# Expert 0's layer 1 in halves of the slots, and vector work reordered around the first gathers, in a routed expert kernel

## What is computed

```
probs  = softmax(rot(x) @ gate_w.T)                 # 4096 x 8; rot mixes the four 128-wide parts of a token
keep   = tokens that pick expert e (top-p 0.9), and that are among the 512 best of e by rank
h      = gelu(rot(x)[kept] @ w1[e].T)               # 512 slots x 512
y      = h @ w2[e].T                                # 512 slots x 512
out    = x + sum over e of probs[:, e] * y[e]       # only for kept tokens
```

## Time and profile before

| | |
|---|---|
| median of 3 runs | 282.74 us (281.26 to 282.98) |
| profiled execution, its own time | 284.87 us |
| its span, first to last instruction | 283.1 us |
| PE busy in the span | 244.9 us, 87% |
| DVE busy | 208.1 us, 74% |
| ACT busy | 151.8 us, 54% |
| POOL busy | 144.5 us, 51% |
| mean granted clock of TensorE | 0.916 of full speed |

### The profile page before, as it was taken

How to read it: one execution, slowest core, us unless ns; L and a number is a source line. 1 busy time by engine, 2 the same in 40 slices (tenths; PEclk the granted TensorE clock), 3 DMA queues, 4 the chain that set the end, 5 groups by cost and what they waited for, 6 DMA issues and landing times.

```text
span 283.1 us, 3852 instructions
## 1 busy us (share of the span) xinstructions
PE 244.9 (87%) x1326; PEld 183.9 (65%) x1326; DVE 208.1 (74%) x505; ACT 151.8 (54%) x281; POOL 144.5 (51%) x104
## 2 busy tenths in 40 slices
PE   0868858665489999999999999999999999999980
PEld 0645423212248888788888888888888888888760
DVE  5299977998955897799789779869977966951330
ACT  6331205686134774676587377468657746754200
POOL 0000000000877258858867885885888587583521
PEclk9995868675759999999999999999999999999997
DMA  6999989910348026925973792594498259054520
GB/s 233 426 424 416 495 306 389 335 47 2 111 128 356 3 74 211 263 48 147 320 128 86 289 220 47 170 300 83 111 312 171 77 208 162 8 77 67 148 111 37
DMA packets 12482, 53.38 MB, mean 189 GB/s; under 512 B 2720, under 2 KB 2976, under 8 KB 9248
## 3 DMA queue, kind: packets, MB, share of 16 engines
q1 hardware_dynamic: 4208, 35.31, 34.1%
q0 software_dynamic: 8256, 17.85, 28.0%
HBM read 44.63 MB, written 17.96 MB: 221 GB/s over the span
## 4 chain that ended last, share of the span: by engine, by line
PE 73%; DVE 13%; DMA 4%; ACT 3%; issue 3%; POOL 2%; POOLq 0%; SPq 0%; ACTq 0%; DVEq 0%
PE bank L762 21%; PE bank L763 20%; PE bank L764 20%; PE bank L742 4%; PE bank L824 2%; ACT region L405 2%; DVE xg L589 2%; DMA xg<-in_x,gath 2%; DMA region<-in_xt 2%; DVE region L637 2%; POOL xg L255 1%; PE bank L803 1%; PE bank L758 1%; DVE csum L595 1%; DVE rank L593 1%
## 5 line engine op out<-in xcount | busy, mean ns | idle before, releaser
L255 POOL DMA_INDIRECT xg<-in_x,gath x32 | 51.7, 1617 | 97.4 <-DVE gath L525 69.9
L469 DVE SCALAR_TENSOR_TENSOR w1rot<-w1raw,rot,w1rot 128x512 f32<-128x512 f32 x84 | 63.1, 751 | 5.1 <-ACT w1rot L308 3.1
L270 POOL DMA_INDIRECT out<-ysb,scat x32 | 53.8, 1680 | 19.8 <-DVE ysb L711 8.0
L762 PE MATMUL bank<-w2h,hh 128*128 128x512 f32 x128 | 51.7, 404 | 0.0
L762 PE MATMUL bank<-xh,w1h 128*128 128x512 f32 x128 | 50.9, 398 | 0.0
L763 PE MATMUL bank<-xl,w1h 128*128 128x512 f32 x128 | 50.1, 391 | 0.0
L764 PE MATMUL bank<-w2h,hl 128*128 128x512 f32 x128 | 50.0, 391 | 0.0
L764 PE MATMUL bank<-xh,w1l 128*128 128x512 f32 x128 | 50.0, 390 | 0.0
L763 PE MATMUL bank<-w2l,hh 128*128 128x512 f32 x128 | 49.9, 390 | 0.0
L498 DVE TENSOR_TENSOR hl<-hf,hh 128x512 fp32r<-128x512 f32 x32 | 22.0, 689 | 32.5 <-ACT hh L339 32.5
L335 ACT ACTIVATE hf<-bank 128x512 f32<-128x512 f32 x32 | 19.1, 598 | 40.2 <-PE bank L764 40.2
(11 more groups left out here) (128 smaller groups left out, 331.5 us busy)
## 6 DMA issues: line engine op xcount, KB each, us to landing
region<-in_xt SPq DMA_DIRECT2D x8, 1024.0 KB, 9.1
w1raw<-in_w SPq DMA_DIRECT2D x8, 1024.0 KB, 9.1
w2raw<-in_w SPq DMA_DIRECT2D x8, 1024.0 KB, 4.8
xg<-in_x,gath POOLq DMA_INDIRECT x32, 3.7
score<-probs_scratch,pidx POOLq DMA_INDIRECT x32, 2.8
out<-ysb,scat POOLq DMA_INDIRECT x32, 7.2
ch<-in_ch SPq DMA_DIRECT2D x1, 368.5 KB, 7.8
cf<-in_cf SPq DMA_DIRECT2D x1, 149.0 KB, 2.2
```

Source lines behind the costliest of these rows:

```text
L255: pool.indirect_dma_start(xg[:, s, :], None, x_d, bass.IndirectOffsetOnAxis(gath[:, e, s:s + 1], 0)).then_inc(xg_in[s], 16)
L270: pool.indirect_dma_start(out_d, bass.IndirectOffsetOnAxis(scat[:, e, s:s + 1], 0), ysb[:, s, :], None, compute_op=ALU.add if e < LAST els ...
L469: ins = nc.vector.scalar_tensor_tensor(dst, w1raw[:, e % 2, i, :], rot[:, j, i:i + 1], dst, ALU.mult, ALU.add)
L762: nc.tensor.matmul(dst, ah, bh, start=first, stop=False)
```

## The change

Layer 1 of expert 0 becomes four calls of `layer1_half(n)`: halves 0 and 1 take the slots 0 to 255 (gathers 0 and 1) with the hidden parts 0, 1 and 2, 3, halves 2 and 3 the slots 256 to 511. Each is 24 matmuls with 256 moving columns where `layer1` had 12 with 512. The transposes of gather 3 are put behind half 0 on PE, `count_before(1, 2, E)` behind half 1, `slot_rows(2)` behind half 3. The seven `keep_clock` matmuls become two behind gather 0 and two behind gather 1. On ACT `x_high0(3)` stands behind `hidden(0, 0)` and `rows_out(1, ...)` behind `hidden(0, 1)`. On DVE `slot_tables` writes gath three instructions earlier with a semaphore of its own (`gath_ready`), one quarter of w1's low part is put ahead of `slot_tables(0)`, the first three `x_low0` go ahead of `count_tokens(2, E)`, `x_low0(3)` behind it and ahead of `w2_low(0)`, and within expert 0 each step of `rotate_w1` and the slot work of expert 2 is put one place later among the `h_low`. Experts 1 to 7 keep their order. The dtypes, the number of columns times weights, and the bytes moved are the same.

```diff
--- before.py
+++ after.py
@@ -171,6 +171,11 @@
         pbank, lbank, rbank = bank[1:3], [bank[i] for i in (0, 3, 5, 7)], bank[4]
         fbank, kbank, cbank, obank, dbank = [bank[i] for i in (6, 0, 3, 5)], bank[7], bank[1:3], bank[3], bank[7]
 
+        HALF = CAP // 2
+        halved = lambda a, n: a[:, 2 * (n % 2):2 * (n % 2) + 2, HALF * (n // 2):HALF * (n // 2 + 1)]
+        tiled = lambda a, e, n: halved(a, n) if e == 0 else a[:, n, :]
+        paired = lambda a, e: a.rearrange("p (f n) -> p f n", f=2) if e == 0 else a
+
         starts_of = lambda n, e0, e1: (obank[:, 0:2 * (e1 - e0)] if n == 0 else
                                        dbank[:, 512 - 2 * (e1 - e0):512]).rearrange("p (e m) -> p e m", m=2)
 
@@ -190,7 +195,7 @@
         base_ready, tb_mm = sem("base_ready"), sem("tb_mm")
         incl_ready, off_mm, rows_mm, rows_ready, begin_ready = (
             sem(n) for n in ("incl_ready", "off_mm", "rows_mm", "rows_ready", "begin_ready"))
-        after_ready, v_mm, slots_ready = (sem(n) for n in ("after_ready", "v_mm", "slots_ready"))
+        after_ready, v_mm, gath_ready, slots_ready = (sem(n) for n in ("after_ready", "v_mm", "gath_ready", "slots_ready"))
         xg_in = [sem(f"xg_in{i}") for i in range(S4)]
         score_in = [sem(f"score_in{i}") for i in range(2)]
         xt_mm, x_hi, x_lo = sem("xt_mm"), sem("x_hi"), sem("x_lo")
@@ -248,7 +253,7 @@
         @block.gpsimd
         def _(pool):
             def gather_x(e):
-                pool.wait_ge(slots_ready, e + 1)
+                pool.wait_ge(gath_ready, e + 1)
                 if e >= 1:
                     pool.wait_ge(xt_mm, C4 * e)
                 for s in range(S4):
@@ -256,6 +261,7 @@
                                             bass.IndirectOffsetOnAxis(gath[:, e, s:s + 1], 0)).then_inc(xg_in[s], 16)
 
             def gather_scores(e):
+                pool.wait_ge(slots_ready, e + 1)
                 if e >= 2:
                     pool.wait_ge(y_ev, S4 * (e - 1))
                 for s in range(S4):
@@ -336,7 +342,7 @@
                 act.wait_ge(h_act, n + 1)
                 if e >= 1:
                     act.wait_ge(y_mm, S4 * e)
-                nc.scalar.activation(hh[:, f, :], hf[:, n % 2, :], ACT.Copy).then_inc(h_hi, 1)
+                nc.scalar.activation(tiled(hh, e, f), paired(hf[:, n % 2, :], e), ACT.Copy).then_inc(h_hi, 1)
 
             def y_out(e, s):
                 n = S4 * e + s
@@ -417,17 +423,20 @@
             w2_high(0)
 
             nc.scalar.activation(warm[:, :], cfv("ident")[:, 0:1], ACT.Gelu)
-            for s in range(S4):
-                if s == S4 - 1:
-                    rows_out(1, 2, E)
-                x_high0(s)
+            x_high0(0)
+            x_high0(1)
             w1_first(1, 0)
+            x_high0(2)
             for e in range(E):
                 more = e + 1 < E
                 hidden(e, 0)
+                if e == 0:
+                    x_high0(3)
                 if more:
                     w1_first(e + 1, 1)
                 hidden(e, 1)
+                if e == 0:
+                    rows_out(1, 2, E)
                 if more:
                     w1_high(e + 1, 0)
                 hidden(e, 2)
@@ -495,7 +504,7 @@
             def h_low(e, f):
                 n = F4 * e + f
                 dve.wait_ge(h_hi, n + 1)
-                nc.vector.tensor_tensor(hl[:, f, :], hf[:, n % 2, :], hh[:, f, :].bitcast(FP32),
+                nc.vector.tensor_tensor(tiled(hl, e, f), paired(hf[:, n % 2, :], e), tiled(hh, e, f).bitcast(FP32),
                                         ALU.subtract).then_inc(h_lo, 1)
 
             def slots_after(e):
@@ -517,12 +526,11 @@
                                              cfv("slot").unsqueeze(2).to_broadcast([P, S4, NT]), ALU.is_le))
                 then(nc.vector.tensor_reduce(tabg[:, :], before_slot[:, :, :], AX.X, ALU.add))
                 then(nc.vector.tensor_tensor(tabf[:, :], tabg[:, :], vbank[:, :, NT], ALU.add))
-                nc.vector.scalar_tensor_tensor(tabx[:, :], tabf[:, :], float(N), cfv("slot"), ALU.is_ge, ALU.mult)
+                nc.vector.tensor_scalar(gath[:, e, :], tabf[:, :], float(N - 1), None, ALU.min).then_inc(gath_ready, 1)
                 then(nc.vector.tensor_scalar(tabg[:, :], tabf[:, :], float(N - 1), None, ALU.min))
-
-                nc.vector.tensor_tensor(scat[:, e, :], tabf[:, :], tabx[:, :], ALU.add)
                 nc.vector.tensor_scalar(pidx[:, e, :], tabg[:, :], float(E), float(e), ALU.mult, ALU.add)
-                nc.vector.tensor_copy(gath[:, e, :], tabg[:, :]).then_inc(slots_ready, 1)
+                then(nc.vector.scalar_tensor_tensor(tabx[:, :], tabf[:, :], float(N), cfv("slot"), ALU.is_ge, ALU.mult))
+                nc.vector.tensor_tensor(scat[:, e, :], tabf[:, :], tabx[:, :], ALU.add).then_inc(slots_ready, 1)
 
             def count_tokens(e0, e1):
 
@@ -662,31 +670,39 @@
             count_tokens(0, 2)
             nc.vector.tensor_copy(rows[:, :, :, NT], chv("rowbase").unsqueeze(1).to_broadcast([P, E, 2])).then_inc(rows_ready, 1)
             slots_after(0)
+            w1_low(0, 2, 3)
             slot_tables(0)
             slots_after(1)
-            w1_low(0, 2, C4)
+            w1_low(0, 3, C4)
             slot_tables(1)
+            x_low0(0)
+            x_low0(1)
+            x_low0(2)
             count_tokens(2, E)
+            x_low0(3)
             w2_low(0)
-            for s in range(S4):
-                x_low0(s)
 
 
             for e in range(E):
                 more, later = e + 1 < E, e + 2 < E
                 if e >= 1:
                     w2_low(e)
-                if more:
+                if e >= 1 and more:
                     rotate_w1(e + 1, 0)
-                if later:
+                if e >= 1 and later:
                     slots_after(e + 2)
                 h_low(e, 0)
                 if more:
+                    rotate_w1(e + 1, 1 if e >= 1 else 0)
+                h_low(e, 1)
+                if e >= 1 and later:
+                    slot_tables(e + 2)
+                if e == 0:
+                    slots_after(e + 2)
                     rotate_w1(e + 1, 1)
-                h_low(e, 1)
-                if later:
+                h_low(e, 2)
+                if e == 0:
                     slot_tables(e + 2)
-                h_low(e, 2)
                 if more:
                     rotate_w1(e + 1, 2)
                 h_low(e, 3)
@@ -742,15 +758,12 @@
                         last = nc.tensor.transpose(xbank[j % 2][:, s * P:(s + 1) * P], xg[:, s, j * P:(j + 1) * P], ident)
                     last.then_inc(xt_mm, 1)
 
-            def transpose_x0():
-
-                for s in range(S4):
-                    pe.wait_ge(xg_in[s], 16)
-                    for j in range(C4):
-                        last = nc.tensor.transpose(x0bank(s)[:, j, :], xg[:, s, j * P:(j + 1) * P], ident)
-                    last.then_inc(xt_mm, 1)
-                    if s == S4 - 2:
-                        count_before(1, 2, E)
+            def transpose_x0(s):
+
+                pe.wait_ge(xg_in[s], 16)
+                for j in range(C4):
+                    last = nc.tensor.transpose(x0bank(s)[:, j, :], xg[:, s, j * P:(j + 1) * P], ident)
+                last.then_inc(xt_mm, 1)
 
             def keep_clock(n):
 
@@ -766,8 +779,6 @@
             def layer1(e, f):
                 if f == 0:
                     pe.wait_ge(w1_lo, C4 * (e + 1))
-                    if e == 0:
-                        pe.wait_ge(x_lo, S4)
                 n = F4 * e + f
                 if n >= 2:
                     pe.wait_ge(h_act, n - 1)
@@ -779,6 +790,24 @@
                                          xh[:, j, :], xl[:, j, :], j == 0, j == C4 - 1)
                 last.then_inc(h_mm, 1)
 
+            def layer1_half(n):
+
+                if n == 0:
+                    pe.wait_ge(w1_lo, C4)
+                    pe.wait_ge(x_lo, S4 // 2)
+                if n == 2:
+                    pe.wait_ge(x_lo, S4)
+                if n >= 2:
+                    pe.wait_ge(h_act, n - 1)
+                ns = slice(HALF * (n // 2), HALF * (n // 2 + 1))
+                for i in range(2):
+                    f = 2 * (n % 2) + i
+                    fs = slice(f * P, (f + 1) * P)
+                    for j in range(C4):
+                        last = split_product(hbank[n % 2][:, i * HALF:(i + 1) * HALF], w1h[0][:, j, fs], w1l[0][:, j, fs],
+                                             xh[:, j, ns], xl[:, j, ns], j == 0, j == C4 - 1)
+                last.then_inc(h_mm, 1)
+
             def layer2(e, s):
                 if s == 0:
                     pe.wait_ge(w2_lo, e + 1)
@@ -787,7 +816,10 @@
                     pe.wait_ge(y_ev, n - 1)
                 ss = slice(s * P, (s + 1) * P)
                 for f in range(F4):
-                    if s == 0:
+                    if e == 0:
+                        if f == 0:
```

(30 more changed lines are left out.)

## The result

The changed kernel takes 287.09 us (median of 4 runs, 284.4 to 287.86), the kernel before in the same comparison 282.64 (281.26 to 282.98): a ratio of 1.0133, 95% interval 1.0076 to 1.0189. The forecast was 283.2 with a range of 280.6 to 286.1. Three further comparisons, on the chips 8, 0 and 14, gave 1.0098 [1.0067, 1.0128], 0.9927 [0.9903, 0.995] and 0.9935 [0.9905, 0.9965]. So the sign differs between the comparisons, each of them on a chip of its own, and both have to be explained: why it is slower where before stands at 283 us, and why it is faster where before stands at 286.4. The ratios are estimated from the single runs and differ a little from the quotients of the medians (1.0157 here, inside the interval). Runs over 1.5% above the fastest of the same kernel (three took 413, 600 and 1327 us) are left out of the ratios, not of the medians.

What follows compares the result with a forecast made beforehand. PE was taken as the bound once layer 1 of expert 0 has begun, with its lead mostly waited away on DVE. A 0.4 us gain and 0.85 for a clock fall gave 282.74 + 0.45 = 283.2 us, range 280.6 to 286.1.

Steps and rivals of the forecast that it cites:

- part 1: POOL's gathers of expert 0 start 0.43 us earlier; the four land at 73.9, 75.2, 76.7 and 77.8, not 80.6 for the last.
- part 2: On PE, layer 1 of expert 0 starts with half 0 at 77.7, 7.0 us earlier than before.
- part 3: PE's 96 matmuls of 256 columns take 0.121 us each; half 0 ends near 82.75, PE is done at 92.8.
- the rival of exposed weight loads: 256-column matmuls on PE can't hide their weight loads: 4.0 to 5.0 us slower than before, 287.2; chance 0.12.
- The clock's rise at 82.3: During half 0, PE's clock rises near 82.3, counting only the matmuls from 77.7.
- the early case of the text: PE's clock rises as early as 78.7 if all earlier work counts; half 0 ends 1.6 us sooner, gain up to 1.3.
- part 4: DVE's gapless list of 13.92 us puts `x_low(1, 0)` at 98.62; PE waits, keeping 0.4 of its 3.5 us lead.
- part 5: With moved loads beside them, expert 1's gathers land at 94.4 to 96.6; at 95.0, about 2.2 us of PE's idle time.
- part 6: PE's clock may fall in the roughly 3 us wait between 92.8 and 99.3: price 0 to 2.45, taken as 0.85.
- POOL held by `w2_low(0)`: POOL's second gather of expert 1 stands behind DVE's `w2_low(0)`, 85.3 to 87.6; the last is issued near 90.2.
- Sum: Whole kernel: -0.4 for the lead plus 0.85 for the clock makes +0.45, 283.2 us (span 283.5).

Runs made afterwards that it cites:

- e1: Changed kernel with the loads of w2 (expert 1) and w1 (expert 2) held until two transposes of expert 1 are done: 282.76 us, ratio 0.9974.
- r3: The changed kernel again, unedited, on chip 8 beside the kernel before: 286.25 us, ratio 1.0098.
- r4: The changed kernel again, unedited, on chip 14 beside the kernel before: 284.58 us, ratio 0.9935.
- e4: Changed kernel with `w2_low(0)` ahead of `x_low0(0)` on DVE and the loads released one transpose earlier, after gather 2: 278.48 us, ratio 0.9831.
- e7: Changed kernel with the w1 load for expert 2 issued first, after three transposes, and the w2 load behind it: 282.27 us, ratio 0.9872.
- e2: Changed kernel with 24 unused `keep_clock` matmuls behind `slot_rows(2)`, filling PE's wait: 284.31 us, ratio 1.0014.
- e6: Changed kernel with `w2_low(0)` as four 128x512 instructions instead of one 128x2048: 282.94 us, ratio 0.9868.
- b1: The kernel before, unedited, on chip 8 for a second profile: 282.9 us, ratio 0.9991.
- e8: e4 with `w2_low(0)` also cut in four pieces as in e6, against the kernel before on chip 8: 280.51 us, ratio 0.99.
- r1: The changed kernel again, unedited, on chip 0 beside the kernel before: 284.19 us, ratio 0.9927.

## Why the prediction was wrong

- **Gathers of expert 0 (part 1): right in the main.** Transposes at 73.41, 74.91 and 76.67 (said: 73.9, 75.2, 76.7 to 76.85). No gather was held, the first neither: 0.94 to 1.12 us each, where the text gave the first 1.6.
- **Layer 1 starts at 77.7 (part 2): right**, 77.53 (77.73 by the chain).
- **A step of 0.121 (part 3): right**, 0.12; the rival of exposed weight loads fell.
- **The clock's rise at 82.3: wrong.** It rose at about 78.3, the early case of the text. Half 0 was over at 80.80 and not 82.75, and PE done at 90.8 and not 92.8. It rose 0.7 us behind the first matmul of layer 1, with transposes and `keep_clock` ahead of it; e1, r3 and r4, which are the same up to there, have it 0.3 ahead of that matmul to 1.2 behind. The text's reason, that in before it rose only at 85.5 and not in the stretches with gaps, leaves out that before's granted clock was also 1.00 from 71.9 to 75.3, between stretches at 0.50. The Trainium skill (TensorE: Matmul & The Clock Gate, Part 4) was named beside the late rise; the late rise did not come, and the trace doesn't tell which of the instructions ahead of 78.3 count. PE's 2 us brought the gathers forward too (the last issued at 88.06, said 90.2), but these landed no sooner than said, so PE's wait grew by them.
- **DVE ends the wait, `x_low(1, 0)` at 98.62 (part 4): wrong here, right as the next bound.** DVE's list was summed rightly (13.92 said, 14.1 measured from `x_low0(3)` to the end of `h_low(0, 3)`). It began 1.9 us sooner than said, was done at 96.88 and stood idle for 1.06 us, for ACT and so for the transposes. PE, in its slow matmuls until 102.64, did not wait for `x_low` at all. With the gathers cured (e1, e4, e7) DVE's `x_low` is what ends PE's wait, by 1.3 to 1.55 us.
- **The gathers land at 95.0 (part 5): the step that failed.** Each piece was seen: the second gather held by `w2_low(0)` (said 85.3 to 87.6 for that instruction, it was 83.4 to 85.7), the loads near 87.7 (85.69). But the landing was taken from the earlier trace rows, 4.2 to 6.4 us, where before's loads had started ahead of the gathers; with both loads going out between them the last one took 7.80. So the last was there at 95.86 and not 95.0, though issued 2 us earlier than said, and PE's transposes began at 96.20. PE had been done since 90.81, so the wait was 5.39 in one piece, where the text had 2.2 for this transfer: 2.0 us more by PE's earlier end, 1.2 by the later start of the transposes. From the landing on, the chain is PE's transposes and layer 2 part 0 at the low clock; at the full clock these would have been over at 99.9, as in before.
- **The fall of the clock (part 6): mis-sized.** I took 0.85 and a bound of 2.45, with a wait of 3 us, likely in two pieces. The wait was 5.39 in one, and the fall cost 2.75 (6.44 against 3.69), more than the bound. The clock fell in every profile of the changed kernel, 4.2 to 4.8 us after PE had stopped, at a price of 1.6 to 2.8. e2 takes it away and gets 2.3 us back in D. This is the largest term of the miss, and it follows from the wait of part 5.
- **POOL held by `w2_low(0)`: right.** 3.06 us beside a free gather's 0.95. The Trainium skill (SBUF — State Buffer, Who interferes with whom) infers that such a `tensor_tensor` does not stall descriptor generation. The trace does not agree, and e6 shows that it is the single long instruction that holds it: in four pieces, 0.94 to 1.16.
- **Sum:** +0.45 was said. The spans of the two first profiles differ by 2.66: the lead gave nothing (96.20 against 96.22) where -0.4 was said, and the clock cost 2.75 where 0.85 was. So of the 2.2 us between forecast and profile the clock made 1.9 and the lost lead 0.4 (what follows was 0.1 shorter). By D the difference is 3.3 (32.87 - 29.60), since the first gather started 0.54 earlier; from b1 to r3, on one chip, it is 4.5. The medians say +4.45 and, in the comparison of r3, +3.0.
- **Not foreseen at all:** that before itself takes 3 us more on some chips, in the same stretch, by a delay that the changed kernel's waits cover, and that the changed kernel takes 1.7 to 2.9 us less there. Only both together turn the sign.

## What to carry to other kernels

A lead on the critical engine is worth what its next input allows: list every transfer that the next step needs, and ask what else has been moved to go out beside it. Here the best versions came from moving the two 1 MB loads out of the gathers' way (e4, 0.983 on one chip; e8, 0.99 on another, where the trace accounts for it), not from the split alone. A long vector instruction that may meet a gather should be cut in pieces: otherwise a few tenths of a us decide which gather is held, and for how long. And a gain of 1 to 2% that leaves two engines' lists tight needs more than one chip: 0.983 on one was 1.0005 on another. Last, look where the profiled execution lies among the runs before its rows are taken for the median.

## What the runs showed of the hardware that was not expected

- The last gather of 128 rows lands after about 3.9 us without loads beside it (e1), and after 7.80 to 9.03 us when two loads of 1 MB go out between the gathers, at about 400 GB/s (first profile, r3).
- A gather on POOL is held by a 128x2048 `tensor_tensor` on DVE that began before it (3.06 us, by 0.05 us), and not by one that begins while it runs (0.95 us in r1, r4 and e7).
- On two of the chips the engines that wait for PE at 91 to 95 us go on about 2 to 3 us behind PE's records in four of seven profiles; on the others they go on as the record ends (b1: 91.55 and 91.58).
- Matmuls of 256 columns (f32 in the records) keep a step of 0.12 us, with a weight load recorded at 0.19 for each.
